# Layer 0's row maxima one batch ahead, turned into rows and subtracted by 32-row products

## What is computed

```python
x = x + L0_xattn(layernorm(x), ctx, ctx, Wq, bq, Wk, bk, Wv, bv, Wo, bo)
# inside, per batch:
qh, kh, vh = heads(q @ Wq.T + bq), heads(k @ Wk.T + bk), heads(v @ Wv.T + bv)
scores = einsum('bhqd,bhkd->bhqk', qh, kh) / sqrt(8)
attn   = softmax(scores, axis=-1)        # over the context, with each row's maximum subtracted
out    = einsum('bhqk,bhkd->bhqd', attn, vh) @ Wo.T + bo
x = x + L0_ffn(layernorm(x), waff, W1, b1, W2, b2, threshold)   # the routed experts
```

## Time and profile before

| | |
|---|---|
| median of 3 runs | 811.79 us (810.83 to 816.41) |
| profiled execution | 811.33 us, its span 809.6 us |
| TensorE busy | 761.8 us, 94% of the span |
| VectorE busy | 672.7 us, 83% |
| GpSimd busy | 478.0 us, 59% |
| ScalarE busy | 440.3 us, 54% |

### The profile page before, as it was taken

How to read it: one execution, slowest core, us unless ns; L and a number is a source line. 1 busy time by engine, 2 the same in 40 slices (tenths; PEclk the granted TensorE clock), 3 DMA queues, 4 the chain that set the end, 5 groups by cost and what they waited for, 6 DMA issues and landing times.

```text
span 809.6 us, 28859 instructions
## 1 busy us (share of the span) xinstructions
PE 761.8 (94%) x10843; PEld 642.5 (79%) x10873; DVE 672.7 (83%) x1775; ACT 440.3 (54%) x1078; POOL 478.0 (59%) x912
## 2 busy tenths in 40 slices
PE   8999999998798998899999999999999999999973
PEld 6777777776598996788888888888888888888861
DVE  6888889887756665689999999989999999999866
ACT  4666666656065764445565555645545555555432
POOL 7767678887856774345554655646555465463324
PEclk9999999999999999999999999999999999999996
DMA  8996220000521211121131221231312213122120
GB/s 239 372 352 255 107 87 15 17 21 28 141 76 50 64 51 37 38 64 45 43 84 48 59 74 46 75 57 47 85 46 75 57 45 85 47 60 64 38 44 14
DMA packets 68253, 65.81 MB, mean 81 GB/s; under 512 B 23714, under 2 KB 49042, under 8 KB 68114
## 3 DMA queue, kind: packets, MB, share of 16 engines
q1 hardware_dynamic: 53250, 39.71, 18.2%
q10 hardware_dynamic: 12816, 20.06, 6.7%
q0 software_dynamic: 2048, 4.20, 1.8%
HBM read 35.89 MB, written 24.37 MB: 74 GB/s over the span
## 4 chain that ended last, share of the span: by engine, by line
PE 35%; DVE 29%; DMA 19%; issue 6%; SPq 6%; POOL 2%; ACT 1%; DVEq 1%; ACTq 0%; another core or an unknown queue 0%; POOLq 0%
DMA a_r_all<-a_r_rows 10%; DMA a_r_rows<-a_rT 7%; SPq L1464 6%; DVE a_mxf L2222 4%; PE psum L1039 4%; PE psum L432 4%; PE psum L421 4%; PE psum L414 3%; DVE a_rT L2238 3%; PE psum L1027 3%; DVE a_oT L2247 3%; DVE f_h L2311 3%; DVE f_hm L2317 2%; DVE f_xt L2296 2%; PE psum L403 2%
## 5 line engine op out<-in xcount | busy, mean ns | idle before, releaser
L2079 ACT ACTIVATE a_pT<-psum 128x512 f32<-128x512 f32 x128 | 69.5, 595 | 49.9 <-PE psum L1888 34.0
L720 DVE TENSOR_REDUCE l_mx<-psum 128x4 bf16<-128x512 f32 x128 | 81.8, 681 | 3.5 <-PE psum L403 1.9
L1571 POOL TENSOR_TENSOR f_hd<-f_hmc,a_wmean 128x1 f32<-128x1 f32 x32 | 6.7, 210 | 131.2 <-DVE f_hr L2322 130.0
L1800 PEld LDWEIGHTS psum<-a_cTm,a_Wk 128*128 128x128 f32 x512 | 64.1, 191 | 19.8 <-issue 19.8
L2222 DVE TENSOR_REDUCE a_mxf<-psum 128x8 f32<-128x1024 f32 x64 | 77.4, 1210 | 2.4 <-PE psum L1857 2.4
L1788 PEld LDWEIGHTS psum<-a_xT,a_Wq 128*128 128x128 f32 x512 | 64.4, 192 | 15.3 <-issue 13.9
L552 ACT ACTIVATE l_pT<-psum 128x512 f32<-128x512 f32 x128 | 70.5, 597 | 7.8 <-PE psum L421 7.5
L1565 POOL TENSOR_SCALAR f_hq<-f_ht 128x512 bf16<-128x512 f32 x31 | 60.3, 1945 | 20.0 <-ACT f_ht L2122 19.9
L1867 PE MATMUL psum<-a_qT,a_kT 64*128 64x128 f32 x1024 | 71.0, 279 | 0.0
L1835 PE MATMUL psum<-a_Wv,a_cTm 128*128 128x512 f32 x128 | 70.0, 633 | 0.2
L1800 PE MATMUL psum<-a_cTm,a_Wk 128*128 128x128 f32 x512 | 70.2, 281 | 0.0
(11 more groups left out here) (313 smaller groups left out, 2066.6 us busy)
## 6 DMA issues: line engine op xcount, KB each, us to landing
sorted_x<-r_zeros ACTq DMA_DIRECT2D x12, 1408.0 KB, 7.2
a_r_all<-a_r_rows SPq DMA_DIRECT2D x124, 128.0 KB
e_xt<-sorted_x SPq DMA_DIRECT2D x39, 64.0 KB, 1.8
sorted_y<-e_yt ACTq DMA_DIRECT2D x39, 64.0 KB, 1.6
e_w<-in_E_W1b SPq DMA_DIRECT2D x1, 2064.0 KB
a_cin<-in_ctx SPq DMA_DIRECT2D x32, 64.0 KB, 2.6
out<-f_x SPq DMA_DIRECT2D x32, 64.0 KB, 2.0
x_res<-in_x SPq DMA_DIRECT2D x1, 512.0 KB, 5.5
```

Source lines behind the costliest of these rows:

```text
L720: nc.vector.tensor_reduce(mx[:, s, Q4 * k:Q4 * k + Q4], maxp[k % 2].rearrange("p (h t) -> p h t", h=Q4), AX_X, ALU.max).then_inc(mx_ready, 1)
L1800: last = nc.tensor.matmul(bank[:, i * S:(i + 1) * S], Wk[:, 4 * half + i, :], cTm[:, b % 2, :], start=True, stop=True)
L2079: nc.scalar.activation(pT[:, 2 * half + e, :], tp[e], ACT.Exp, scale=SCALE).then_inc(exp_ready, 1)
```

## The change

- `mx` becomes a tile of 4 groups of 32 columns per batch parity, set to zero once by GpSimd ahead of its first `x_rsqrt`; four columns of each group are used.
- `maxima(b, s, u)` reduces both `maxp` banks at once; it runs twice per batch. All of a batch's maxima are taken in the batch before.
- `maxima_turn(b)`: one product of `mx` with `negI` turns the 128 columns into 128 rows, negative; `turn_copy(b)` (ScalarE) brings them to `mxT` in bf16.
- `minus_max(b)`: 16 products of 32 rows, in turn on the four row groups: a one-hot column `sel` (made by `head_rows`), broadcast, times the group's rows of `mxT`. The exponentials of all four groups become ready together.
- `maxp` takes banks 1 and 2, the first of `tp` bank 5.
- New orders on TensorE, ScalarE and VectorE; `x_stats(b+4)` stands near the end of VectorE's batch.

```diff
--- before.py
+++ after.py
@@ -113,7 +113,8 @@
     qz = sb("l0_qz", [P, 3, Q4, S])
     kT = sb("l0_kT", [P, 3, S])
     v = sb("l0_v", [P, 4, H, 32])
-    mx = sb("l0_mx", [P, 2, H], BF16)
+    mx, mxT = sb("l0_mx", [P, 2, Q4, R], BF16), sb("l0_mxT", [P, 2, S], BF16)
+    sel = sb("l0_sel", [P, Q4], BF16)
     pT = sb("l0_pT", [P, 4, Q4 * S])
     oev = sb("l0_oev", [P, 2, Q4 * S])
     rden = sb("l0_rden", [P, H])
@@ -129,14 +130,15 @@
     xt_done, qkv_done = sem("l0_xt_done"), sem("l0_qkv_done")
     qz_ready, kT_ready, v_ready = sem("l0_qz_ready"), sem("l0_kT_ready"), sem("l0_v_ready")
     max_done, mx_ready = sem("l0_max_done"), sem("l0_mx_ready")
+    mx_set, turn_done, row_ready, sel_ready = sem("l0_mx_set"), sem("l0_turn_done"), sem("l0_row_ready"), sem("l0_sel_ready")
     t_done, exp_ready, pv_done = sem("l0_t_done"), sem("l0_exp_ready"), sem("l0_pv_done")
     oev_ready, outp_done, on_ready = sem("l0_oev_ready"), sem("l0_outp_done"), sem("l0_on")
     oT_ready = sem("l0_oT_ready")
     x1_stats = sem("l0_x1_stats")
 
     xp, yp = psum[:, 0, :], psum[:, 6, :]
-    maxp = [psum[:, i, :] for i in (1, 5)]
-    tp = [psum[:, i, :] for i in (2, 3, 4, 7)]
+    maxp = [psum[:, i, :] for i in (1, 2)]
+    tp = [psum[:, i, :] for i in (5, 3, 4, 7)]
     xnp, nump = (xp[:, 0:S], maxp[0][:, 0:S]), (xp[:, S:S + E], maxp[1][:, 0:E])
     placep = xp[:, S + 64:S + 64 + 8 * E]
     countp = xp[:, S + 16:S + 16 + E]
@@ -271,6 +273,7 @@
                 out=dram["xs"], out_offset=bass.IndirectOffsetOnAxis(ap=rt["pos_s"][:, r:r + 1].bitcast(U32), axis=0),
                 in_=xn2[:, r, :], in_offset=None).then_inc(rsem["scat"], 16)
 
+        nc.gpsimd.memset(mx[:], 0.0).then_inc(mx_set, 1)
         x_rsqrt(0, 0)
         nc.gpsimd.memset(v[:, 0, :, HD:], 1.0).then_inc(rsem["set"], 1)
         x_rsqrt(1, 1)
@@ -414,13 +417,22 @@
                 nc.tensor.matmul(tp[k], kT[r, b % 3, :], qz[r, b % 3, :, :].rearrange("p h q -> p (h q)"), start=True, stop=False,
                                  skip_group_check=True)
 
-        def minus_max(b, k):
-            pe.wait_ge(mx_ready, 4 * b + k + 1)
+        def maxima_turn(b):
+            pe.wait_ge(mx_ready, 4 * b + 4)
+            nc.tensor.matmul(maxp[0][:, 0:S], mx[:, b % 2, :, :].rearrange("p k j -> p (k j)"), negI[:],
+                             start=True, stop=True).then_inc(turn_done, 1)
+
+        def minus_max(b):
+            pe.wait_ge(row_ready, b + 1)
+            if b == 0:
+                pe.wait_ge(sel_ready, 1)
             for j in range(Q4):
-                h = Q4 * k + j
-                last = nc.tensor.matmul(tp[k][:, j * S:(j + 1) * S], mx[:, b % 2, h:h + 1].to_broadcast([P, P]),
-                                        negI[:], start=False, stop=(j == Q4 - 1), skip_group_check=True)
-            last.then_inc(t_done, 1)
+                for k in range(Q4):
+                    r = slice(R * k, R * (k + 1))
+                    last = nc.tensor.matmul(tp[k][:, j * S:(j + 1) * S], sel[r, j:j + 1].to_broadcast([R, P]), mxT[r, b % 2, :],
+                                            start=False, stop=(j == Q4 - 1), skip_group_check=True)
+                    if j == Q4 - 1:
+                        last.then_inc(t_done, 1)
 
         def values(b):
             wait(pe, x1_stats, 3 * (b - 1) + 1)
@@ -459,42 +471,36 @@
         idle_products(2)
         projections(1, 1)
         max_scores(0, 0)
-        scores(0)
-        minus_max(0, 0)
         max_scores(0, 1)
         for b in range(B):
             s, more = b % 2, b + 2 < B
-            if b >= 1:
-                scores(b)
-                minus_max(b, 0)
+            scores(b)
+            maxima_turn(b)
             if b >= 4:
                 route_transpose(b - 4)
             if b in close_at:
                 places(close_at[b])
+            if b >= 1:
+                back_transposes(b - 1, 1 - s)
+            if b >= 4:
+                affinity(b - 4)
+            minus_max(b)
+            if b + 1 < B:
+                max_scores(b + 1, 0)
+            if more:
+                x_transpose(b + 2, s)
             if b == 0:
                 expert_sums()
             else:
-                back_transposes(b - 1, 1 - s)
-            minus_max(b, 1)
-            if b >= 4:
-                affinity(b - 4)
-            if b + 1 < B:
-                max_scores(b + 1, 0)
-            if b >= 1:
                 o_transpose(b - 1, 1 - s)
             if more:
-                x_transpose(b + 2, s)
-            minus_max(b, 2)
-            minus_max(b, 3)
+                projections(b + 2, s)
             if b >= 1:
                 output(b - 1, 1 - s)
-            if more:
-                projections(b + 2, s)
-            values(b)
             if b + 1 < B:
                 max_scores(b + 1, 1)
-            else:
-                route_transpose(B - 4)
+            values(b)
+        route_transpose(B - 4)
         affinity(B - 4)
         back_transposes(B - 1, 1)
         route_transpose(B - 3)
@@ -546,6 +552,11 @@
             wait(act, pv_done, 4 * (b - 3))
             nc.scalar.copy(v[:, b % 4, :, 0:HD], (first_v[b] if b < 2 else xp)[:, 3 * S:4 * S].rearrange("p (h d) -> p h d", h=H)).then_inc(v_ready, 1)
 
+        def turn_copy(b):
+            act.wait_ge(turn_done, b + 1)
+            wait(act, t_done, 4 * (b - 1))
+            nc.scalar.copy(mxT[:, b % 2, :], maxp[0][:, 0:S]).then_inc(row_ready, 1)
+
         def exps(b, s, k):
             act.wait_ge(t_done, 4 * b + k + 1)
             wait(act, pv_done, 4 * b + k - 3)
@@ -573,12 +584,15 @@
         nc.scalar.activation(rt["wsq"][:], rt["waffT"][:], ACT.Square).then_inc(rsem["wsq"], 1)
         for b in range(B):
             s, first, more = b % 2, b == 0, b + 2 < B
+            turn_copy(b)
+            if b >= 4:
+                route_copy(b - 4)
             exps(b, s, 0)
-            exps(b, s, 1)
+            if more:
+                x_copy(b + 2, s)
             if not first:
                 o_copy(b - 1, 1 - s)
-            if more:
-                x_copy(b + 2, s)
+            exps(b, s, 1)
             exps(b, s, 2)
             exps(b, s, 3)
             if more:
@@ -591,8 +605,7 @@
             if b == B - 1:
                 after_exps()
             pv_copy(b, s)
-            if b >= 3:
-                route_copy(b - 3)
+        route_copy(B - 4)
         route_copy(B - 3)
         o_copy(B - 1, 1)
         for r in range(B - 2, B):
@@ -713,12 +726,18 @@
             locate_rows(q)
             locate_position(q)
 
-        def maxima(b, s, k):
-            dve.wait_ge(max_done, 4 * b + k + 1)
-            if k == 0:
-                wait(dve, t_done, 4 * (b - 1))
-            nc.vector.tensor_reduce(mx[:, s, Q4 * k:Q4 * k + Q4], maxp[k % 2].rearrange("p (h t) -> p h t", h=Q4),
-                                    AX_X, ALU.max).then_inc(mx_ready, 1)
+        def maxima(b, s, u):
+            dve.wait_ge(max_done, 4 * b + 2 * u + 2)
+            if b == 0:
+                dve.wait_ge(mx_set, 1)
+            if u == 0:
+                wait(dve, turn_done, b - 1)
+            nc.vector.tensor_reduce(mx[:, s, 2 * u:2 * u + 2, 0:Q4], psum[:, 1:3, :].rearrange("p e (h t) -> p e h t", h=Q4),
+                                    AX_X, ALU.max).then_inc(mx_ready, 2)
+
+        def head_rows():
+            dve.wait_ge(cst, consts["n_ready"])
+            nc.vector.tensor_reduce(sel[:], ident[:].rearrange("p (k r) -> p r k", k=Q4)[:, 0:Q4, :], AX_X, ALU.max).then_inc(sel_ready, 1)
 
         def normalise(b, s):
             dve.wait_ge(outp_done, 3 * b + 1)
@@ -753,10 +772,9 @@
         q_spread(0, 0)
         q_spread(1, 1)
         maxima(0, 0, 0)
+        x_stats(2, 0)
         maxima(0, 0, 1)
-        x_stats(2, 0)
-        maxima(0, 0, 2)
-        maxima(0, 0, 3)
+        head_rows()
         x_stats(3, 1)
         for b in range(B):
             s, more = b % 2, b + 2 < B
@@ -772,24 +790,22 @@
                 normalise(b - 1, 1 - s)
             if b >= 4:
                 num_copy(b - 4)
-            if b + 4 < B:
-                x_stats(b + 4, s)
             if b + 1 < B:
                 maxima(b + 1, 1 - s, 0)
-                maxima(b + 1, 1 - s, 1)
             if b >= 1:
                 residual(b - 1, 1 - s)
             if b - 4 in group_at and SPREAD <= group_at[b - 4] < NG - 2:
                 choose(group_at[b - 4])
+            if b + 1 < B:
+                maxima(b + 1, 1 - s, 1)
+            if more:
+                q_spread(b + 2, s)
             for q in range(SPREAD):
                 choose_spread(q, b - GROUPS[q][1] - 2)
             if b in close_at and close_at[b] < SPREAD:
                 locate_position(close_at[b])
-            if more:
-                q_spread(b + 2, s)
-            if b + 1 < B:
-                maxima(b + 1, 1 - s, 2)
-                maxima(b + 1, 1 - s, 3)
+            if b + 4 < B:
+                x_stats(b + 4, s)
             if b == B - 1:
```

## The result

| | before | changed |
|---|---|---|
| median | 813.75 us (810.83 to 816.41, 4 runs) | 823.52 us (820.38 to 825.38, 4 runs) |
| profiled execution, its span | 811.33, 809.6 | 824.89, 822.8 |
| ratio of the two | | 1.0138, 95% interval 1.0096 to 1.0180 |

The changed kernel is slower by 1.4%, 9.8 us. The forecast was 817 us (5.2 over the median of 811.8 shown then), its range 806 to 826. The time lies in the range, but above the 811 to 821 that the likeliest case gave itself, and beyond 1%: the sum was +5.6, and it came out at 1.75 times that.

The account below looks back on a forecast made before the run. It took a loop through three engines to lead TensorE in layer 0, and GpSimd to set the end from about batch 25. 0.8+1.8+1.4-0.8+2.4 = +5.6 on 811.3 gave 816.9, taken as 817; range 806 to 826.

Parts of the forecast that it names:

- likeliest case: The forecast itself: terms summing to +5.6, time 817 us, between 811 and 821; chance 0.45.
- batches 1 to 3: Layer 0, batches without affinity and route_copy: period 5.36 by the walk against 5.62 before; -0.8 us.
- walk: One layer 0 batch step by step in the new order: period 5.8 against 5.76, +0.8 over batches 4 to 24.
- choose_spread: VectorE, ten batches: now ahead of x_stats instead of in a pause, 0.2 late on average; +1.8 us.
- Subtraction: minus_max on TensorE: 16 full-row products, 0.9 in all, become 16 of 32 rows taking 0.24, bound 0.42.
- rate-bound rival: minus_max: 32-row products bound by rate, 26 ns each, 0.42 instead of 0.24; +4.3, 821 us; chance 0.28.
- 3 x 0.22, from 3.38 to 4.04: Walk step on TensorE: projections, now ahead of output, run from 3.38 to 4.04 after the batch's scores start.
- rival of the shorter loop: Stall at affinity and handovers are taken at full; without them 5.6 a batch, 5 less: 812 us; chance 0.13.
- First batches: Start of layer 0: values of batch 0 later by 1.3 through wide maxima, memset +0.1; together +1.4 us.
- GpSimd: GpSimd's queue: x_norm(28) 3.05 later, a 0.64 pause absorbs part; +2.4 us at the end of layer 0.
- Time given back: Rival: TensorE is the bound, 0.78 saved per batch, 18.7 over 24 batches; 797 us; chance 0.14.

Follow-up runs that it names:

- second pair of profiles: Both kernels without edits, each in a second profiled execution; changed 821.15 us, ratio 1.0159; before 808.52 us, ratio 0.9991.
- Output_first: Changed kernel with output(b-1) ahead of projections(b+2) on TensorE; 826.86 us, ratio 1.0174 to the kernel before.
- x_early: Changed kernel with x_transpose right behind the turn, x_copy behind turn_copy, minus_max ahead of places and affinity, route_transpose in another bank; 816.22 us, ratio 1.0041.
- Affinity_later: Changed kernel with affinity of an ordinary batch behind minus_max on TensorE instead of ahead of it; 825.43 us, ratio 1.0188.
- stats_early: Changed kernel with x_stats(b+4) moved into VectorE's pause between the first maximum and the residual; 820.46 us, ratio 1.0105.
- late_choose: Changed kernel with VectorE's choose of the third group, in batch 27, behind the second maximum and q_spread; 821.57 us, ratio 1.0111.
- fill_both: Changed kernel with 12 idle products in TensorE's waits of batch 0 and 17 more in batch 28's; 822.66 us, ratio 1.0112.
- fill_start: Changed kernel with 12 idle products (identity times itself) in TensorE's waits of batch 0; 822.96 us, ratio 1.0128.
- group_by_group: Changed kernel with the 16 products of minus_max issued one row group after the other; 825.72 us, ratio 1.0161.

## Why the prediction was right or wrong

The second pair of profiles against the sum:

| stretch | before | changed | difference | forecast |
|---|---|---|---|---|
| to the scores of batch 1 | 15.89 | 17.45 | +1.56 | +1.4 |
| batches 1 to 3 | 16.86 | 16.42 | -0.44 | -0.8 |
| batches 4 to 24 | 122.80 | 128.29 | +5.49 | +0.8 and +1.8 |
| batch 25 to the last scatter | 62.06 | 64.88 | +2.82 | +2.4 |
| sum, layer 0 | 217.61 | 227.04 | +9.43 | +5.6 |
| behind it | 586.9 | 590.2 | +3.3 | 0 |

The medians differ by 9.8 in the first measurement and by 12.6 in the second; the 9.4 of layer 0 accounts for most of either, and the 3.3 behind it is less than the 6.6 that one kernel shows between two executions. The first pair differs more in the stretches where its clock differed: +3.29, +1.39, +5.53 and +5.27, together +15.5, and -2.3 behind it.

The sum itself was rounded down: its walk gives 5.81 less 5.76, 0.05 in each of 21 batches, and ten times 0.2 for choose_spread, which is 0.4 more than the +0.8 and +1.8 that it adds up.

- *Subtraction.* Right: 16 products start within 0.19 and end 0.40 after the first start, against about 0.45 forecast; the 0.65 of the rate-bound rival is refuted. The Trainium skill, page TensorE: Matmul & The Clock Gate, Part 3, says that products on different tiles start about 4 ns apart; the records agree (four starts within 0.01), and the floor of about 25 ns in its Part 1 doesn't hold for them.
- *The walk.* Each step up to the start of the projections is within 0.03: turn 1.07, back_transposes 1.26 (1.24), affinity 1.83 (1.85), minus_max 2.15 (2.12), x_transpose 2.70, exps 0 2.58, x_copy 3.07, projections 3.39 (3.38). **The step that failed is "3 x 0.22, from 3.38 to 4.04".** The duration came from the earlier trace rows, where k follows other work without a pause. Here TensorE has waited 0.24 for x_copy, and k takes 0.32 to its successor: output starts at 4.16, values at 4.93 instead of 4.80, the period is 5.94 instead of 5.81. Output_first moves those 0.10 to output, and x_early, where nothing is waited for, has 0.22 again. 0.13 more in 21 batches is +2.7, and 0.11 in three makes the -0.8 a -0.44. I had charged every wait, but not what follows one; the rival of the shorter loop erred to the other side.
- *Why the loop is what it is.* The forecast blamed minus_max, exps 0, x_copy and the projections. Affinity_later shows that minus_max and exps 0 are not it alone: with both 0.35 earlier the period grew, because x_copy also hangs on num_copy and x_transpose. That the x side's place costs the gain is shown by x_early, 0.18 a batch; it also moves minus_max ahead of affinity, but that alone, in affinity_later, cost 0.13.
- *choose_spread.* +1.8 forecast; 5.49 less 21 x 0.18 leaves 1.7, and stats_early takes 1.6 of it away.
- *First batches.* +1.4 against +1.56, right at full clock. That the clock could fall there I hadn't forecast; in the first profile it adds 3.5 by batch 25. Whether it falls there more often than in the kernel before, and what it does to the medians, isn't shown: six profiles of nine against none of two are too few.
- *GpSimd.* The lag is there: x_norm(28) at +1.54 (forecast +1.3), scatters up to 212.87 later by 12.8, that is by 2.6 more than batch 25. But the conclusion "what TensorE does between 25 and 31 lies under this and costs nothing more" was wrong. Its 2.4 came near the second pair's +2.82, but the first pair has +5.27, so that was in part luck. The premise was misread already in the kernel before: the chain of waits at the end of layer 0 (start, us, what) lies on TensorE and VectorE up to 192.4, batch 28 and its choose included, and passes to GpSimd only there:

```profile
192.42 0.23 POOL r_vpe L238
...
201.41 0.58 POOL r_rs L240
202.02 0.35 DVE xy L746
```

In the changed kernel the scatter at 218.41 waits 3.66 for VectorE's positions (1.69 in the second execution). The same scatter before:

```profile
203.40 1.08 POOL L270 DMA_INDIRECT sorted_x<-xy,r_pos_s  x1 [1.42 <-DVE r_pos_s L710]
```

These 1.42 are no slack: the chain above runs from GpSimd's own r_rs over VectorE's xy to the positions, so a late GpSimd passes its lag on. What is over 1.42 is another path. The chain of the changed kernel runs over TensorE (at half clock from 214.2 to 221.1) and ScalarE:

```profile
218.01 0.27 ACT l_oT L573
218.33 0.79 PE psum L462 x2
```

Where batch 28 is short, the forecast's path comes back. In late_choose and fill_both it takes 10.5, the wait is 1.42 again, and the chain lies on GpSimd from 168 to 207. From batch 25 to the last scatter they need 63.8 and 63.7, 3.1 more than the 60.6 of the first execution before. So the lag does cost something near the 2.4, but on top of it comes what batch 28 takes beyond some 10.5.
- *Chances.* "Time given back" named the x side as what stands in its way, rightly, but with it out only 7 of the 10 us come back: the next loop takes 5.76, and the rival's 797 is not reached. That a third case, the forecast with a larger size, crosses 1% was in the range and had too little of the chance.

What stays open: how much a half clock in batch 28 costs on its own (late choose and idle products both shorten the batch, to 10.54 and 10.47, and both also have less half clock there), and how often it falls in batch 0 over many executions.

## What to carry to other kernels

A product that is removed from TensorE is worth what the loop it lies in gives back, so before forecasting, find which copies stand between an engine's last use of a bank and the next batch; here the x side cost the gain, and moving it brought the time back. Price an operation from a row that stands where yours will stand: one that follows a wait is dearer than one in a stream. Follow the queue that is said to set the end to its very last wait, and take a profile twice before a difference of a few us between two of them is explained.

## What the runs showed of the hardware

- An f32 product of 128 rows (two passes, x2 in the rows) that follows 0.16 to 0.41 of idle time on TensorE takes 0.49 instead of 0.39 and its successor starts 0.32 behind it instead of 0.22, at full clock. All eight profiles in which k waits for x_copy show it on k (both of changed, fill_start, fill_both, group_by_group, stats_early, affinity_later, late_choose), output_first shows it on output.
- Sixteen products of 32 rows and 128 columns on four row groups take 0.40 from first start to last end when issued in turn over the groups and 0.43 group by group.
- With the same waits to 0.01 us in batch 0, one execution fell to 1.2 GHz for 10.2 us and another of the same kernel stayed at 2.4. With the waits filled it stayed up in three profiles of three, without in three of nine. The kernels' whole times (fill_start 822.96, fill_both 822.66) show no gain from it.
- A scores group of eight took 2.09 at 1.2 GHz and 1.14 at 2.4.
